# The D stage of a recursive feature-interaction kernel: group order, copies on two engines, stores on two queues, a later weight load

## What is computed

```python
def _L0_rec_ref(inputs, W0, W1, W2, b0, b1, b2, lin_w, lin_b):   # inputs (512, 40, 16), W0 (40,40,100), W1, W2 (40,100,100)
    Ws, bs = [W0, W1, W2], [b0, b1, b2]
    base = curr = inputs
    logit = []
    for Wk, bk in zip(Ws, bs):
        z = jnp.einsum('bid,bjd->bdij', base, curr)
        curr = jnp.einsum('bdij,ijh->bhd', z, Wk) + bk[None, :, None]
        logit.append(curr)
    pooled = jnp.sum(jnp.concatenate(logit, axis=1), axis=-1)
    return pooled @ lin_w + lin_b
```

## Time and profile before

| | us |
|---|---|
| median of 3 runs | 185.82 |
| lowest, highest | 185.5, 186.17 |
| the profiled execution | 186.29 |
| its span (first to last instruction) | 184.5 |
| TensorE busy | 175.8 (95%) |
| VectorE busy | 151.8 (82%) |
| ScalarE busy | 73.9 (40%) |
| GpSimd busy | 16.2 (9%) |

### The profile page before, as it was taken

How to read it: one execution, slowest core, us unless ns; L and a number is a source line. 1 busy time by engine, 2 the same in 40 slices (tenths; PEclk the granted TensorE clock), 3 DMA queues, 4 the chain that set the end, 5 groups by cost and what they waited for, 6 DMA issues and landing times.

```text
span 184.5 us, 2573 instructions
## 1 busy us (share of the span) xinstructions
PE 175.8 (95%) x814; PEld 118.7 (64%) x814; DVE 151.8 (82%) x135; ACT 73.9 (40%) x79; POOL 16.2 (9%) x21
## 2 busy tenths in 40 slices
PE   7798998869999999999999999999999999999994
PEld 2364474546677777777777777777777777777760
DVE  0699698869999999999999999999999999300622
ACT  2554664124444624462446244534453445002001
POOL 3670010087000000000000000000000000000000
PEclk9999999999999999999999999999999999999999
DMA  6999997999797739774986597659765200000000
GB/s 192 379 409 411 412 219 218 231 406 397 230 324 233 234 122 321 247 227 124 331 230 228 126 322 235 223 135 329 228 219 128 99 0 0 0 0 4 0 0 0
DMA packets 11845, 37.71 MB, mean 204 GB/s; under 512 B 2305, under 2 KB 2941, under 8 KB 11838
## 3 DMA queue, kind: packets, MB, share of 16 engines
q1 hardware_dynamic: 11538, 37.38, 62.1%
q0 software_dynamic: 48, 0.16, 0.3%
q10 hardware_dynamic: 252, 0.09, 0.3%
HBM read 36.28 MB, written 1.33 MB: 204 GB/s over the span
## 4 chain that ended last, share of the span: by engine, by line
PE 79%; DMA 8%; SPq 3%; POOL 3%; issue 2%; DVE 1%; ACT 1%; DVEq 0%; ACTq 0%
PE q_ps L434 39%; PE c_ps L434 36%; DMA pair_sb<-d_dram 3%; DMA pair_sb<-w_pairs 3%; DMA d_dram<-w_d 2%; PE q_ps L518 2%; SPq L153 2%; POOL pair_sb L401 1%; POOL wq_low L424 1%; PE q_ps L443 1%; POOL wc_low L406 1%; DVE xb_z L246 1%; ACT z_high L324 1%; SPq L159 1%; PE c_ps L565 1%
## 5 line engine op out<-in xcount | busy, mean ns | idle before, releaser
L324 ACT ACTIVATE z_high<-xb_z 126x1024 fp32r<-126x1024 f32 x56 | 59.2, 1060 | 73.0 <-DVE xb_z L246 69.3
L253 DVE TENSOR_TENSOR z_low<-xb_z,z_high 126x1024 fp32r<-126x1024 f32 x56 | 68.9, 1232 | 1.1 <-ACT z_high L324 0.8
L246 DVE TENSOR_TENSOR xb_z<-x_a,xb_z 126x1024 f32<-126x1024 f32 x50 | 62.1, 1242 | 8.3 <-DMA xb_z<-xw 8.3
L434 PE MATMUL q_ps<-z_high,wq_high 126*101 126x512 f32 x108 | 34.1, 396 | 3.0 <-POOL wq_low L424 1.5
L434 PE MATMUL c_ps<-z_high,wc_high 126*101 126x512 f32 x112 | 35.5, 398 | 0.2 <-issue 0.2
L434 PE MATMUL c_ps<-z_high,wc_low 126*101 126x512 f32 x112 | 35.0, 394 | 0.0
L434 PE MATMUL c_ps<-z_low,wc_high 126*101 126x512 f32 x112 | 35.0, 394 | 0.0
L434 PE MATMUL q_ps<-z_high,wq_low 126*101 126x512 f32 x108 | 33.8, 394 | 0.0
L434 PE MATMUL q_ps<-z_low,wq_high 126*101 126x512 f32 x108 | 33.7, 393 | 0.0
L434 PEld LDWEIGHTS q_ps<-z_high,wq_high 126*101 126x101 f32 x108 | 17.7, 165 | 10.8 <-POOL wq_low L424 2.0
L434 PEld LDWEIGHTS c_ps<-z_high,wc_high 126*101 126x101 f32 x112 | 18.0, 165 | 9.0 <-issue 1.6
(11 more groups left out here) (56 smaller groups left out, 66.1 us busy)
## 6 DMA issues: line engine op xcount, KB each, us to landing
xb_z<-xw SPq DMA_DIRECT2D x50, 512.0 KB, 4.5
x_a<-xa SPq DMA_DIRECT2D x8, 512.0 KB, 5.0
w_d<-w2h SPq DMA_DIRECT2D x4, 512.0 KB, 7.4
w_post<-w1x SPq DMA_DIRECT2D x3, 512.0 KB, 10.0
d_dram<-w_d SPq DMA_DIRECT2D x4, 252.5 KB, 4.3
w_post<-w1x SPq DMA_DIRECT2D x1, 562.5 KB, 12.7
pair_sb<-d_dram SPq DMA_DIRECT2D x6, 82.9 KB
pair_sb<-w_pairs SPq DMA_DIRECT2D x1, 404.0 KB, 5.4
```

What stands on the lines that cost most here:

```text
L246: nc.vector.tensor_tensor(xb_z[0:K, c, :], x_a[0:K, u % 2, :], x_b, ALU.mult).then_inc(z_done, 1)
L253: nc.vector.tensor_tensor(z_low[0:K, m % SLOTS, :], xb_z[0:K, c, :], z_high[0:K, m % SLOTS, :].bitcast(fp32), ALU.subtract).then_inc(low_d ...
L324: nc.scalar.activation(z_high[0:K, m % SLOTS, :], xb_z[0:K, m % C, :], ACT.Copy).then_inc(high_done, 1)
L434: last = nc.tensor.matmul(ps[0:J, h * B:(h + 1) * B], w[0:K, c * J:(c + 1) * J], z[0:K, slot, h * B:(h + 1) * B], start=(c == 0 and k == 0 ...
```

## The change

- **Order of the groups.** TensorE does group 4 (the short one) first, then 0, 1, the selecting matmul 6, then 2, 3. c1 is now behind all of them (before: between groups 1 and 2). The loads of w1 come in the order 4, 0, 1, 2, 3, group 4 as a load of its own.
- **Copies.** ScalarE copies groups 4, 0, 2; VectorE copies 1 (ahead of form5) and 3 (behind form5).
- **Stores.** SP issues the stores of the lower half, ScalarE those of the upper half (two of them), and the one that GpSimd issued goes to SP.
- **Loads.** The third piece of `w0_pairs` is loaded last of the weights, behind w1, and its rounding on ScalarE stands behind ScalarE's second store. The load of x_a for unit 1 stands between the first and second group of stores, the load of x_b for m = 7 behind all stores. The loads for m = 8 and 9 are behind `d_stored`, between the gathers; those for 10 to 13 behind the last gather.
- **q weights.** VectorE takes chunks 0, 1 behind form7 (before: form9), and also chunks 2, 3, behind form9; GpSimd keeps 4 to 6. split6 comes ahead of form7, split7 behind `first_weights(0)`, split8 behind form8.

The core of the diff:

```diff
-W1_CUTS = (0, 1, 2, 3, NG)
+W1_CUTS = (0, 1, 2, 3, 4, NG)
+W1_ORDER = (4, 0, 1, 2, 3)
+D_ORDER = (4, 0, 1, 2, 3)
-DS = 6
+DS = 7
-PREP_AT = 9
-GATHER_AT = 8
+PREP_AT = (7, 9)
+GATHER_AT = 7
...
             for side, t, piece in GATHER:
                 if piece == 1 and (side, t) == (0, 0):
-                    sp.wait_ge(low_done, 4)
-                    load_xb(1, 3)
+                    sp.wait_ge(low_done, 2)
+                    load_xb(1, 1)
+                if piece == 1 and (side, t) == (1, 1):
+                    sp.wait_ge(low_done, 3)
+                    load_xb(1, 2)
...
+            def copy_d(g):
+                dve.wait_ge(dgroup_done, D_ORDER.index(g) + 1)
+                nc.vector.tensor_copy(w2_d[:, g * GI * J:(g + 1) * GI * J], d_ps[0]).then_inc(dgroup_copied_dve, 1)
...
                 for m in range(m0, m0 + BODY):
+                    if m == 5:
+                        copy_d(1)
+                    if m == C:
+                        split(it, C - 1)
                     form(it, m)
+                    if m == 5:
+                        copy_d(3)
...
-                    if m == PREP_AT:
-                        first_weights()
-                    if m > 1:
+                    if m == PREP_AT[0]:
+                        first_weights(0)
+                        split(it, C)
+                    elif m == C + 1:
+                        split(it, m)
+                    elif m == PREP_AT[1]:
+                        first_weights(1)
+                    elif m > 1:
                         split(it, m - 1)
...
+            copy_d(4)
             copy_d(0)
-            copy_d(1)
             round_high(0, 4)
+            act.wait_ge(dgroup_copied, 2)
+            act.wait_ge(dgroup_copied_dve, 1)
+            store_d(act, 1, LEFT + LOWER, 0, 2 * GI, (0, DR))
             copy_d(2)
-            copy_d(3)
-            copy_d(4)
-            act.wait_ge(dgroup_copied, NG)
+            act.wait_ge(dgroup_copied, 3)
+            act.wait_ge(dgroup_copied_dve, 2)
+            store_d(act, 1, LEFT + LOWER + 2 * GI, 2 * GI, 2 * GI, (0, DR))
+            cast_w0(2)
...
             turn_v()
+            d_group(4)
             d_group(0)
             d_group(1)
-            c1_chunk(0, 1)
+            select_xb(6)
             d_group(2)
             d_group(3)
-            select_xb(6)
-            d_group(4)
-            for m in range(2, LAG):
+            for m in range(1, LAG):
                 c1_chunk(0, m)
```

More of the change, by code:

```diff
@@ L20 @@
 PRODUCT_AT = 20
-C1_AT = 3 * C - LAG
+C1_AT = 2 * C - 1
 VP = 4
@@ L209, in _ @@
-            load_xb(1, 2)
+            load_w0(2)
+            sp.wait_ge(dgroup_copied, 1)
+            store_d(sp, 0, LEFT + 4 * GI, 4 * GI, LOWER - 4 * GI, (0, DR))
+            sp.wait_ge(dgroup_copied, 2)
+            sp.wait_ge(dgroup_copied_dve, 1)
+            store_d(sp, 0, LEFT, 0, 2 * GI, (0, DR))
+            store_d(sp, 0, LEFT + F, 0, RIGHT, (32, DR))
+            load_xa(1, 1)
+            sp.wait_ge(dgroup_copied, 3)
+            sp.wait_ge(dgroup_copied_dve, 2)
+            store_d(sp, 0, LEFT + 2 * GI, 2 * GI, 2 * GI, (0, DR))
@@ L217, in _ @@
                 if side == 0 or piece > 0:
                     gather_d(sp, side, t, piece)
-            for c in range(4, C):
+            for c in range(3, C):
                 sp.wait_ge(low_done, c + 1)
@@ L336, in copy_d, with cast_w0 @@
                 rows, n = (2 * DR, GI * J) if g < NG - 1 else (DR, J)
-                act.wait_ge(dgroup_done, g + 1)
-                nc.scalar.activation(w2_d[0:rows, g * GI * J:g * GI * J + n], d_ps[g % 2][0:rows, 0:n],
+                act.wait_ge(dgroup_done, D_ORDER.index(g) + 1)
+                nc.scalar.activation(w2_d[0:rows, g * GI * J:g * GI * J + n], d_ps[D_ORDER.index(g) % 2][0:rows, 0:n],
                                      ACT.Copy).then_inc(dgroup_copied, 1)
+            def cast_w0(i):
+                act.wait_ge(wc_sums, i + 1)
+                nc.scalar.activation(chunks(wc_high, WC_CUTS[i], WC_CUTS[i + 1]),
+                                     w0_sides[0:K, WC_CUTS[i]:WC_CUTS[i + 1], 0, :], ACT.Copy).then_inc(wc_highs, 1)
             act.wait_ge(xa_loaded[0], 16)
@@ L345, in _ @@
             nc.scalar.activation(select_r[:, :], select_sb, ACT.Copy).then_inc(select_rounded, 1)
-            for i in range(len(WC_CUTS) - 1):
-                act.wait_ge(wc_sums, i + 1)
-                nc.scalar.activation(chunks(wc_high, WC_CUTS[i], WC_CUTS[i + 1]),
-                                     w0_sides[0:K, WC_CUTS[i]:WC_CUTS[i + 1], 0, :], ACT.Copy).then_inc(wc_highs, 1)
+            cast_w0(0)
+            cast_w0(1)
             round_high(0, 1)
@@ L370, in _ @@
                     act.wait_ge(d_stored, 16 * DS)
-                    act.wait_ge(d_stored_pool, 16)
                     for t in range(T):
@@ L506, in d_group @@
             def d_group(g):
-                if g == 0:
+                place = D_ORDER.index(g)
+                d_bank = d_ps[place % 2]
+                if place == 0:
                     pe.wait_ge(v_copied, 1)
-                if g == 1:
+                if place == 1:
                     pe.wait_ge(const_copied, 1)
-                if g in W1_CUTS:
-                    pe.wait_ge(w1_loaded[W1_CUTS.index(g)], 16)
-                if g >= 2:
-                    pe.wait_ge(dgroup_copied, g - 1)
+                pe.wait_ge(w1_loaded[g], 16)
+                if place == 2:
+                    pe.wait_ge(dgroup_copied, 1)
+                if place == 3:
+                    pe.wait_ge(dgroup_copied, 2)
+                if place == 4:
+                    pe.wait_ge(dgroup_copied_dve, 1)
                 n = (GI if g < NG - 1 else 1) * J
                 first = g * GW
-                last = nc.tensor.matmul(d_ps[g % 2][0:DR, 0:n], v_sb[:, :], w1_post[0:J, first:first + n],
+                last = nc.tensor.matmul(d_bank[0:DR, 0:n], v_sb[:, :], w1_post[0:J, first:first + n],
                                         start=True, stop=True)
                 if g < NG - 1:
-                    last = nc.tensor.matmul(d_ps[g % 2][DR:2 * DR, 0:n], v_sb[:, :],
+                    last = nc.tensor.matmul(d_bank[DR:2 * DR, 0:n], v_sb[:, :],
                                             w1_post[0:J, first + n:first + 2 * n], start=True, stop=True)
```

70 lines of the change are left out of this document (29 added, 41 removed).

## The result

| | before | changed |
|---|---|---|
| median, us | 186.0 (4 runs, 185.5 to 187.82) | 190.8 (4 runs, 189.4 to 192.2) |
| profiled execution | 186.29 | 189.4 |
| its span | 184.5 | 187.6 |

The ratio is 1.024, 95% interval 1.0134 to 1.0346: slower by 4.8 us in the medians and by 3.1 in the profiled pair. The forecast was 187.7 with a range up to 189.4, so the direction held and the size did not: the median lies above the range.

A forecast was written before the change was run, and what follows sets the result against it. The loop is full, so q4's start decides, set by the store and gather chain with VectorE close behind. q4 at 48.1 against 46.23, +1.9, takes the profiled 186.29 to 188.2, median 187.7; range 185.3 to 189.4.

The forecast's parts named there:

- What bounds the kernel, and where the loss appears: Loop full at 100 of 100 us; only when q4 starts counts, and VectorE's lost time before split9 or split10 delays TensorE.
- The D stage: Group matmuls and copies: two VectorE copies at 0.6 us each, falling where VectorE waited anyway; net about +0.1 us to VectorE.
- Stores and gathers: Stores issued 1.0 us earlier land at 27.4, a gain of 0.6; gathers go out then and first weights start at 31.2.
- rival (a): The two store queues don't help, stores land at 28.3, q4 at 49.1, +2.9: 188.7 us; chance 0.22.
- The new place of the wait: split7 behind first weights, c7 ahead of q0: TensorE idle 29.7 to 33.4, q0 at 34.8 instead of 33.10, +1.7.
- Up to q4: VectorE from split7 at 32.2 to split9's end at 41.1, then c9, q2 at 42.5 and q4 at 48.1, +1.9.
- GpSimd's hindrance: VectorE slowed ahead of split9 while GpSimd runs its three remaining operations, two VectorE operations affected: 0.4 us.
- From the profile to the median: Profiled execution forecast at 188.2 us, taken to lie 0.47 above the median, giving 187.7.
- Rival (c), the clock: TensorE's granted clock halves to 1.2 GHz for a few chunks after the wait ahead of c7: +2 to +3, 190.3; chance 0.06.
- Rival (b), faster: Stores land at 26.0, split9 done at 39.2, q4 at 46.2: same, 185.8, or faster if split9 ends earlier; chance 0.24.

The follow-up runs named there:

- the fill: Changed kernel with 12 bf16 matmuls of zeros in TensorE's wait ahead of c7: 192.34 us, ratio 1.0368.
- the two split7 experiments: Changed kernel with split7 ahead of the first weights on VectorE: 191.81 us; the same with the m = 7 x_b load ahead of all stores: 191.58 us.
- GpSimd with chunks 2 and 3: Changed kernel with the q weights of chunks 2 and 3 back on GpSimd, as in the kernel before: 189.87 us, ratio 1.0218.
- order alone: Changed kernel, D stage and VectorE's order kept, with the x_a and x_b loads issued where the kernel before has them: 190.17 us, ratio 1.0207.
- LAG 7: Changed kernel with LAG = 7 instead of 8, so c7 comes behind q0: 188.87 us, ratio 1.0158.
- early load: Changed kernel with split7 ahead of the first weights and the m = 7 x_b load issued ahead of all stores: 191.58 us, ratio 1.029.
- D stage alone: Changed D stage only, with loads, VectorE's list around the q weights and GpSimd's share as in the kernel before: 185.51 us, ratio 0.999.
- loads alone: Changed D stage and loads, with before's VectorE order except second weights on VectorE behind split9: 192.71 us, ratio 1.0357.
- the better kernel: Changed D stage with before's loads and VectorE order, second weights on VectorE behind split9: 185.49 us; with GpSimd's chunks 4 to 6 held behind split10: 185.01 us.

## Where the prediction held and where it failed

- **What bounds the kernel, and where the loss appears.** Held. The loop is untouched, TensorE waited ahead of c7 (foreseen 3.7, measured 2.96), c9 waited 1.94 for split9 and q2 did not wait for its weights.
- **The D stage.** Held. A copy on VectorE cost 0.60 from start to start (18.31 to 18.91), as taken. One thing was missed without harm: c1 waited 0.88 us for GpSimd's part of its weights, and c7's wait took that up.
- **Stores and gathers.** Held in the profiled execution, with some luck: gathers at 27.68 (foreseen 27.4), first weights at 30.92 (31.2). Over all the profiled executions here the gathers went out at 26.50 to 28.26, the last all but rival (a)'s 28.3, so 0.3 us from the foreseen value says little of the reasoning. That the change moves the landing at all no run shows.
- **The new place of the wait.** Held: c7 at 33.23 (33.4), q0 at 35.21 (34.8; the difference is the clock).
- **"Up to q4".** This step failed. It gave VectorE 32.2 to 41.1, 8.9 us, and it took 10.5. Two terms were wrong. The wait of 1.12 us of split8 for ScalarE was absent from the sum: the order of instructions showed form8 and split8 side by side, before's profile has ScalarE's rounding at 1.06 a chunk, and I put the two at VectorE's rate. That 1.12 (or 1.13) was read in each trace with this order and in none with the other; no run took it away alone. And GpSimd's hindrance was put at 0.4, from two operations met by three; it was 1.34 (0.71 in the second weights, 0.63 in form10), because the small operations suffer as well. The two excesses, 2.06, less 0.5 of load waits that didn't come, give the 1.6. The start was 0.3 early, so split9 ended 1.3 late, q4 came at 49.48 instead of 48.1, and the profiled execution took 189.4 instead of 188.2.
- **From the profile to the median.** This added 1.9 more. I took the profiled execution to lie 0.47 above the median; it was the fastest of the four, 1.4 below it: 189.4, with the others at 190.28, 191.31 and 192.2. Why is open, since those three have no trace. Two things are at hand. In the profiled executions with this order the first weights start anywhere from 30.92 to 32.02, and with VectorE's list as the bound that goes through to the end, 1.1 us at most. And the mean granted clock was 0.991 and 1.00 in the two faster executions but 0.982 in the two slower; in the traces of the fill and of the two split7 experiments a second drop, behind c9, cost 1.5 to 1.6 us. Both together would cover the 2.8 between the fastest and the slowest, but 0.982 was also read for one long drop (GpSimd with chunks 2 and 3), which cost less.
- **Rival (c), the clock.** The drop happened, given 0.06. Its price of 2 to 3 us on top did not follow in the profiled execution, since c9 waits for split9 whether c7 to q1 are fast or slow. That its 190.3 lies near the measured 190.8 is luck. Behind c9 nothing hides a drop, and there the rival may have come true in the slower executions, which no trace shows.
- **Rival (b), faster.** Refuted at its own point: split9 had to end by 39.2 and ended at 42.4.

## What to carry to other kernels

When an engine's list has a wait for a long DMA chain, list what stands behind the wait, and count each of those operations on the path; moving the weights two chunks forward saved none of the chain and put three operations of 1.15 us behind it (split7, form8, split8), for which the kernel with the order alone had all the data. Where two operations on one tile stand side by side in an engine's list and another engine works on the tile between them, add that operation as a bubble. And when two waits follow each other, removing or filling the first only helps if the second does not take it over.

## What the runs showed of the hardware

- After TensorE waits of 1.99 (LAG 7, ahead of q0), 2.18 (early load, c7), 2.38 (D stage alone, c1), 2.73 to 2.96, 3.08, 3.19, 3.55 and 3.77 us the granted clock went to 0.50 (1.2 GHz), for about 3 us in the changed kernel and more than 6 after the 3.77, and a chunk took up to 2.66 us in place of 1.4. It is not a matter of the wait's length alone: after one of 2.01 (order alone, ahead of c9), the changed kernel's of 1.94 and before's of 1.50 the chunks ran at full speed. With the first wait filled, TensorE stood longer ahead of c9 (2.85 us), and the drop came there.
- A drop cost next to nothing where another engine bounds the stretch (c7 to q1 in the changed kernel), 1.5 to 1.6 us behind c9, and some 2.5 behind q0 with the loads alone.
- Stores to DRAM ended in a tail of about 1 us at a quarter of the DMA engines' share and less, and were signalled some 0.7 us after that.
- Beside GpSimd's three operations, VectorE's cast of 126x202 went from 0.27 to 0.79 us, its subtraction from 0.37 to 0.57, its product of 1024 columns from 1.22 to 1.86. Moving the GpSimd work behind the critical stretch gave split9 1.0 us earlier in the changed kernel; in the medians it is 1.2 us there and 0.5 in the better kernel, each with overlapping intervals.
